# A gated cross-attention block on one core: values laid out by token in device memory, scores laid out by head and query

## The reference

```python
def attention(hidden_q, hidden_kv, mask, bias, Wq, Wk, Wv, Wo):   # 32 heads of 128
    q, k, v = (hidden_q @ Wq, hidden_kv @ Wk, hidden_kv @ Wv)     # reshaped to b, 64, 32, 128
    score = einsum('bqhd,bkhd->bhqk', q, k) / sqrt(128) + bias
    probs = softmax(where(mask, score, -inf));  probs = where(mask, probs, 0)
    return einsum('bhqk,bkhd->bqhd', probs, v).reshape(b, 64, 4096) @ Wo

x = x + tanh(g_xattn) * attention(layernorm(x), ctx, ...)
x = x + tanh(g_ffn) * ffn(layernorm(x), ...)   # ffn: low-rank scores choose one of each 32
                                               # hidden units (1792 in all), relu, product with w2t
```

## Time and profile before

| | |
|---|---|
| median of 3 runs | 1898.65 us (1897.91 to 1899.12) |
| the profiled execution | 1899.45 us, span 1897.7 us |
| mean granted clock of TensorE | 0.992 of full |
| busy: PE, PEld, DVE, ACT, POOL | 98%, 84%, 58%, 37%, 50% |
| bytes moved by DMA | 329.88 MB in 185,597 packets |
| loads of kt, qt (2048 KB each), 16 of each | 8.9 us and 13.8 us from issue to landing |
| loads of v (512 KB each), 64 | 11.2 us from issue to landing |

### The profile page before, as it was taken

How to read it: one execution, slowest core, us unless ns; L and a number is a source line. 1 busy time by engine, 2 the same in 40 slices (tenths; PEclk the granted TensorE clock), 3 DMA queues, 4 the chain that set the end, 5 groups by cost and what they waited for, 6 DMA issues and landing times. The chain is left out here.

```text
span 1897.7 us, 37889 instructions
## 1 busy us (share of the span) xinstructions
PE 1853.6 (98%) x15304; PEld 1594.9 (84%) x15304; DVE 1095.4 (58%) x1748; ACT 698.7 (37%) x1773; POOL 958.0 (50%) x762
## 2 busy tenths in 40 slices
PE   8999999999999999999989999999999889999999
PEld 7899988799998888888868888888888668888887
DVE  5333466333355455334357777877777877777673
ACT  4233333322233333333345555555555432222221
POOL 5666688766668788778723232323323432111110
PEclk9999999999999999999999999999999999999999
DMA  5555665644455554467679998799985430000000
GB/s 178 168 179 170 194 207 187 200 161 152 144 184 188 189 189 166 166 225 244 200 232 319 294 254 249 221 319 307 253 263 144 131 122 23 23 23 27 25 17 17
DMA packets 185597, 329.88 MB, mean 174 GB/s; under 512 B 11856, under 2 KB 118480, under 8 KB 176464
## 3 DMA queue, kind: packets, MB, share of 16 engines
q1 hardware_dynamic: 185424, 327.47, 54.9%
HBM read 214.17 MB, written 113.25 MB: 173 GB/s over the span
## 5 line engine op out<-in xcount | busy, mean ns | idle before, releaser
L1409 PE MATMUL bank<-tokens_hi,wkq_hi 128*128 128x512 f32 x888 | 347.1, 391 | 4.9 <-DVE tokens_lo L1014 3.3
L1410 PE MATMUL bank<-tokens_lo,wkq_hi 128*128 128x512 f32 x888 | 345.8, 389 | 0.0
L1411 PE MATMUL bank<-tokens_hi,wkq_lo 128*128 128x512 f32 x888 | 345.8, 389 | 0.0
L685 POOL TENSOR_TENSOR wkq_lo<-raw_wkq,wkq_hi 128x768 fp32r<-128x768 f32 x126 | 284.1, 2274 | 122.0 <-ACT wkq_hi L791 121.7
L1409 PE MATMUL bank<-wv_s_hi,tokens_hi 128*128 128x256 f32 x896 | 255.6, 285 | 4.1 <-POOL wv_s_lo L685 4.1
L1410 PE MATMUL bank<-wv_s_lo,tokens_hi 128*128 128x256 f32 x896 | 254.8, 284 | 0.0
L1411 PE MATMUL bank<-wv_s_hi,tokens_lo 128*128 128x256 f32 x896 | 254.7, 284 | 0.0
L1409 PE MATMUL bank<-wo_hi,attn_t_hi 128*128 128x512 f32 x512 | 207.6, 405 | 12.3 <-DVE attn_sum L1208 7.2
L1411 PE MATMUL bank<-wo_hi,attn_t_lo 128*128 128x512 f32 x512 | 201.4, 393 | 0.0
L1409 PEld LDWEIGHTS bank<-tokens_hi,wkq_hi 128*128 128x128 f32 x888 | 166.7, 188 | 40.7 <-issue 4.7
L1410 PE MATMUL bank<-wo_lo,attn_t_hi 128*128 128x512 f32 x512 | 200.9, 392 | 0.0
(11 more groups left out here) (145 smaller groups left out, 3729.1 us busy)
## 6 DMA issues: line engine op xcount, KB each, us to landing
k_t<-c SPq DMA_DIRECT2D x128, 256.0 KB, 2.4
v_by_head<-c SPq DMA_DIRECT2D x128, 256.0 KB, 2.2
q_t<-c SPq DMA_DIRECT2D x128, 256.0 KB, 2.4
kt<-k_t SPq DMA_DIRECT2D x16, 2048.0 KB, 8.9
qt<-q_t SPq DMA_DIRECT2D x16, 2048.0 KB, 13.8
v<-v_by_head SPq DMA_DIRECT2D x64, 512.0 KB, 11.2
raw_wkq<-in_wk SPq DMA_DIRECT2D x32, 512.0 KB, 4.0
raw_wv<-in_wv SPq DMA_DIRECT2D x16, 1024.0 KB, 5.6
```

The costliest lines, as they stand in the source:

```text
L685: pool.tensor_tensor(lo, job_raw(r)[:, a:b, :], hi.bitcast(F32), ALU.subtract)\
L1409: pe.matmul(o, a[0], b[0], start=first_mm, stop=False, skip_group_check=not grouped)
L1410: pe.matmul(o, a[0], b[1], start=False, stop=False, skip_group_check=not grouped)
L1411: return pe.matmul(o, a[1], b[0], start=False, stop=last_mm, skip_group_check=not grouped)
```

## The change

The values lie in device memory by token (`v_by_token`): for each iteration 128 rows (token of a pair) of 8 pairs x 4 heads x 128 float32, 16 KB in a row. One DMA loads an iteration. For that, the score tile is laid out anew: its partitions are (one of two heads, query of a batch), and its columns (couple of heads, batch of the pair, key). The transposes then give partitions (batch, key), which is a token. The bias is laid out accordingly on input. The mask now depends on the column and, for both heads, the query; it comes as three inputs: by row (for the row factor) and by query for each half. Since the two heads of a partition share a query but the two batches do not, the row factor no longer fits the partition: it is multiplied into the gate of the final sum instead (`gate_valid`). The order of score and value matmuls follows the layout; their number and sizes are the same. In SP's order the mask loads come behind a wait for the stores of the normalised tokens, in whose buffer's place the new mask tiles lie; `mask_add[1]` takes the place of `mask_rows` and of its own input `mask_in[1]`.

```diff
-    v_d = nc.dram_tensor("v_by_head", [ITERS, PPH, P, 2, 2, DH], F32, kind="Internal").ap()
+    v_d = nc.dram_tensor("v_by_token", [ITERS, P, PPH, 2, 2 * DH], F32, kind="Internal").ap()
...
-        mask_add = at("mask_add", [P, PAIRS, S], BF16, 0.5)
+        mask_add = [at(f"mask_add{i}", [P, PPH, 2, S], BF16, (204, 0.5)[i]) for i in range(HALVES)]
-        mask_in = at("mask_in", [P, PAIRS, S], U8, 206)
+        mask_in = [at(f"mask_in{i}", [P, PPH, 2, S], U8, (206, 205)[i]) for i in range(HALVES)]
+        mask_rows = at("mask_by_row", [P, PAIRS, S], U8, 204)
...
@@ store @@
-                    dst = v_d[half * G + u // 2, t:t + 2, :, i].rearrange("t q h d -> q t (h d)")
+                    dst = v_d[half * G + u // 2, :, t:t + 2, i, :]
@@ load_v @@
-                for h in range(2):
-                    for i in range(2):
-                        sp.dma_start(v[it % 2][h * S:(h + 1) * S, :, :, i, :].rearrange("k p b d -> k (p b) d"),
-                                     v_d[it][:, :, i, h, :].rearrange("p (b k) d -> k (p b) d", b=2))\
-                            .then_inc(v_in[it % 2], 16)
+                sp.dma_start(v[it % 2][:, :, :, :], v_d[it].rearrange("q t i e -> q t (i e)"))\
+                    .then_inc(v_in[it % 2], 16)
@@ SP, n == 83 @@
-                    sp.dma_start(mask_in[:, :, :], mask).then_inc(mask_sem, 16)
+                    sp.wait_ge(xn_out, 16 * PAIRS)
+                    sp.dma_start(mask_rows[:, :, :], mask[:, 0:PAIRS * S].rearrange("p (t k) -> p t k", k=S))\
+                        .then_inc(mask_sem, 16)
+                    for i in range(HALVES):
+                        ...
@@ ACT @@
-                hi = cxo[d % 2][0][:, :, :, :].rearrange("p a (r h) t -> p h a r t", h=2)[:, h]
+                hi = cxo[d % 2][0][:, :, :, h * S:(h + 1) * S]
...
-                if n == 90:
+                if n == 86:
                     act.wait_ge(gate_sem, 16)
                     act.activation(gate[:, :], gate_in[:, :], ACT.Tanh).then_inc(act_gate, 1)
@@ masks @@
-                dve.wait_ge(mask_sem, 16)
-                dve.tensor_scalar(mask_add[:, :, :], mask_in[:, :, :], -MASKED, MASKED, ALU.mult, ALU.add)\
-                    .then_inc(dve_mask, 1)
-                dve.tensor_reduce(valid[:, :], mask_in[:, :, :], AX.X, ALU.max).then_inc(dve_mask, 1)
+                dve.wait_ge(mask_sem, 48)
+                dve.tensor_reduce(valid[:, :], mask_rows[:, :, :], AX.X, ALU.max).then_inc(dve_mask, 1)
+                dve.tensor_scalar(mask_add[1][:, :, :, :], mask_in[1][:, :, :, :], -MASKED, MASKED,
+                                  ALU.mult, ALU.add).then_inc(dve_mask, 1)
+                dve.wait_ge(dve_mask, 2)
+                dve.tensor_scalar(mask_add[0][:, :, :, :], mask_in[0][:, :, :, :], -MASKED, MASKED,
+                                  ALU.mult, ALU.add).then_inc(dve_mask, 1)
+                dve.wait_ge(act_gate, 1)
+                dve.tensor_scalar(gate_valid[:, :], valid[:, :], gate[:, 0:1], None, ALU.mult).then_inc(dve_mask, 1)
@@ probs, DVE @@
-                dve.scalar_tensor_tensor(
-                    out=sc[s % 2][:, :, :], in0=sc[s % 2][:, :, :], scalar=valid[:, tile:tile + 1],
-                    in1=rinv[s % 2][:, :].unsqueeze(2).broadcast_to([P, HG, S]),
-                    op0=ALU.mult, op1=ALU.mult).then_inc(dve_p, 1)
+                dve.tensor_tensor(sc[s % 2][:, :, :], sc[s % 2][:, :, :],
+                                  rinv[s % 2][:, :].unsqueeze(2).broadcast_to([P, HG, S]), ALU.mult)\
+                    .then_inc(dve_p, 1)
@@ scores, PE @@
-                    for h in range(HG):
-                        o = (s % 2 * HG + h) * S
-                        for q in range(2):
-                            cols = slice(p * P + q * S, p * P + (q + 1) * S)
-                            mm = pe.matmul(bank[SCORE_BANK[r % 2]][q * S:(q + 1) * S, o:o + S],
-                                           qt[it % 2][:, h, cols], kt[it % 2][:, h, cols], start=True, stop=True)
+                    for r_ in range(2):
+                        for b in range(2):
+                            cols = slice(p * P + b * S, p * P + (b + 1) * S)
+                            o = (s % 2 * HG + 2 * r_ + b) * S
+                            for h in range(2):
+                                mm = pe.matmul(bank[SCORE_BANK[r % 2]][h * S:(h + 1) * S, o:o + S],
+                                               qt[it % 2][:, 2 * r_ + h, cols], kt[it % 2][:, 2 * r_ + h, cols],
+                                               start=True, stop=True)
@@ attend, PE @@
-                for b in range(2):
-                    for r in range(2):
-                        o = (s % 2 * 4 + 2 * r + b) * S
-                        for i in range(4):
-                            a, h = divmod(i, 2)
-                            keys = slice(h * S, (h + 1) * S)
...
+                for h in range(HG):
+                    o = (s % 2 * HG + h) * S
+                    for i in range(4):
+                        a, b = divmod(i, 2)
+                        keys = slice(b * S, (b + 1) * S)
...
```

More of the change, by code:

```diff
@@ L173, in build @@
         valid = tiny("row_has_key", [P, PAIRS], F32, 64)
+        gate_valid = tiny("gate_if_key", [P, PAIRS], F32, 64)
         m1 = tiny("block_max", [P, NBLK], F32, 224)
@@ L203, in build @@
         qt = [at(f"qt{i}", [P, HG, 2 * TB], F32, (20, 76)[i]) for i in range(2)]
-        v = [at(f"v{i}", [P, PPH, 2, 2, DH], F32, (36, 92)[i]) for i in range(2)]
+        v = [at(f"v{i}", [P, PPH, HG, DH], F32, (36, 92)[i]) for i in range(2)]
         bias_in = [at(f"bias_in{i}", [P, PPH, HG * S], F32, (52, 108)[i]) for i in range(2)]
@@ L593, in _ @@
                     sp.dma_start(gate_in[:, :], gates).then_inc(gate_sem, 16)
-                    sp.dma_start(mask_in[:, :, :], mask).then_inc(mask_sem, 16)
+                    sp.wait_ge(xn_out, 16 * PAIRS)
+                    sp.dma_start(mask_rows[:, :, :], mask[:, 0:PAIRS * S].rearrange("p (t k) -> p t k", k=S))\
+                        .then_inc(mask_sem, 16)
+                    for i in range(HALVES):
+                        o = (i + 1) * PAIRS * S
+                        sp.dma_start(mask_in[i][:, :, :, :],
+                                     mask[:, o:o + PAIRS * S].rearrange("p (t b k) -> p t b k", b=2, k=S))\
+                            .then_inc(mask_sem, 16)
                 if n == 86:
@@ L701, in do_bm @@
                 if s == 0:
-                    pool.wait_ge(dve_mask, 2)
+                    pool.wait_ge(dve_mask, 4)
                 if p == 0:
                     pool.wait_ge(*loaded(bias_sem, it))
[L705 to L708, removed]
+                b = bias_in[it % 2][:, p, :].rearrange("p (r k) -> p r k", r=2)
+                m = mask_add[it // G][:, p, :, :].rearrange("p b k -> p (b k)")
+                pool.tensor_tensor(b, b, m.unsqueeze(1).broadcast_to([P, 2, 2 * S]), ALU.add).then_inc(pool_bm, 1)
             def do_lo(n):
@@ L1106, in probs @@
             def probs(s):
-                it, p = divmod(s, PPH)
-                tile = PPH * (it // G) + p
                 dve.wait_ge(act_exp, s + 1)
@@ L1189, in clo @@
                 dve.wait_ge(act_chi, 2 * d + h + 1)
-                hi, lo = (t[:, :, :, :].rearrange("p a (r h) t -> p h a r t", h=2)[:, h] for t in cxo[d % 2])
-                dve.tensor_tensor(lo, bank[PV_BANK[h]][:, :].rearrange("p (a r t) -> p a r t", a=2, r=2),
+                hi, lo = (t[:, :, :, h * S:(h + 1) * S] for t in cxo[d % 2])
+                dve.tensor_tensor(lo, bank[PV_BANK[h]][:, :].rearrange("p (a h q) -> p a h q", a=2, q=S),
                                   hi.bitcast(F32), ALU.subtract).then_inc(dve_clo, 1)
@@ L1211, in add_wo @@
                     dve.wait_ge(dve_wo, s + 1)
-                    dve.scalar_tensor_tensor(out=acc[:, p, :], in0=acc[:, p, :], scalar=gate[:, 0:1],
+                    dve.scalar_tensor_tensor(out=acc[:, p, :], in0=acc[:, p, :], scalar=gate_valid[:, tile:tile + 1],
                                              in1=xres[tile % 2][:, :], op0=ALU.mult, op1=ALU.add)\
@@ L1301, in finish @@
                     .then_inc(dve_o, 1)
-            dve.wait_ge(act_gate, 1)
+            dve.wait_ge(dve_mask, 4)
             for d in range(DUOS + 3):
@@ L1503, in attend @@
                     pe.wait_ge(dve_clo, s)
-                for b in range(2):
-                    for r in range(2):
-                        o = (s % 2 * 4 + 2 * r + b) * S
-                        for i in range(4):
-                            a, h = divmod(i, 2)
-                            keys = slice(h * S, (h + 1) * S)
-                            dims = slice(a * S, (a + 1) * S)
-                            mm = pe.matmul(bank[PV_BANK[h]][dims, o:o + S], v[it % 2][keys, p, b, r, dims],
-                                           pt[keys, s % 2, r, b, :], start=True, stop=True)
+                for h in range(HG):
[3 more added lines that the diff above has]
```

(13 more changed lines are left out.)

8 lines of the change are left out of this document (4 added, 4 removed).

## The result

After: 1901.26 us median of 21 runs (1898.02 to 1904.16); before, beside them on the same chip: 1898.65 (1895.66 to 1900.42). The ratio is 1.0017 [1.0011, 1.0023]: the change costs 2.6 us, where the forecast was a gain of 2.0. The profiled execution took 1901.21.

A forecast was written before the change was run, and what follows sets the result against it. TensorE, busy 98% of the span, was taken as the bound, so only less matmul work or shorter seams pay. -1.97 - 0.15 + 0.1 = -2.0 us from the 1898.65 median gave 1896.6, called "same"; stated range 1891.5 to 1902.

The forecast's parts named there:

- Masks at unit 88: VectorE's added mask work ahead of u2 and u3, about +0.9 us there, stalls TensorE 0 to 0.3: +0.1 taken.
- The slack of 0.9: At unit 88, u3 could end about 0.9 us later before TensorE's matmuls would have to wait.
- +0.6 for writing in place: At unit 88, 0.6 us more if the mask product writing over its own input's place ran at half speed.
- Holes, -1.97: Two gaps in the value matmuls near 1290, read as late instructions during DMA backlog, would go: -1.97 us.
- Rival A: The gaps in the value matmuls near 1290 stay: 1898.6 us; chance 0.21.
- C: Late instructions become more frequent in the value matmuls while v flows in 16 KB packets: about 1912 us; chance 0.11.
- D: The new order of score matmuls does not overlap in pairs, +74 us: about 1970; chance 0.03.
- Row factor, -0.15: Probabilities product (L1112) without its per-partition factor: 0.06 us less each, -0.15 for TensorE at the seams.
- B: The last seam, after 1500, shortens too, with less wait for the attention sum: about 1892 us; chance 0.18.
- The middle one: Seam at 1250 to 1300: VectorE's x-tile wait stays, as v is not ahead of it in SP's queue: 0.
- Stores, score and value matmuls, 0: Stores of v land well before their buffer is reused; score and value matmuls keep number and alternation: 0 each.
- slower: The outcome of a measurably slower kernel: chance 0.16, made of C, D and 0.02.

The follow-up runs named there:

- masks apart: Kernel after with the mask work behind u3, second product and gate_valid in unit 89: 1898.01 us against 1899.02 before, ratio 0.9994.
- reduction first: Kernel before with only the reduction put ahead of its one mask product: a single run of 1900.29 us.
- GpSimd in pieces: Kernel after with GpSimd's subtractions in units 86 to 92 cut into pieces of 128x256: 1898.8 us, ratio 1.0 to before.

## Why the prediction was wrong

**Failed: "Masks at unit 88", +0.1 forecast, +4.87 measured.** I priced the second product at the 0.69 of the first, and the 128x16 one with its wait at 0.2: a block of 2.19 + 0.9 = 3.1. It is 6.25. The slack of 0.9 that I had worked out was right: 6.25 - 2.19 = 4.06 later, less 0.9, is 3.2, and TensorE's next matmul came 3.16 late; the second expense, 1.7 at the lower clock behind the idle, I hadn't thought of. What was missing is that the one row I took the price from the earlier trace rows was a lucky one, placed between two operations of GpSimd, and that the change moves the products off that place by putting the reduction ahead of them. I never read GpSimd's rows there, and bounded the term only by a +0.6 for writing in place, which neither product does. The Trainium skill (SBUF — State Buffer, SBUF: two separate sides, and Who interferes with whom) has the rule: VectorE and GpSimd share a port pair, held for a whole instruction; a tensor_scalar in a two-port mode and a GpSimd operation block each other fully, a tensor_reduce and ScalarE are outside it. The traces agree as far as they show it: products that end half a microsecond behind GpSimd's operations, reductions of 1.22 in every kernel, 1.05 on ScalarE. The mode that a product runs in stands in no row.

**Holes, -1.97: right in kind, smaller as a rule.** Transposes of the kernel after, where two duos had taken 18.41 us:

```profile
1291.49 0.66 PE L1499 MATMUL bank<-ident,scores 128*128 128x128 f32 x4
...
1299.71 0.66 PE L1499 MATMUL bank<-ident,scores 128*128 128x128 f32 x4
```

8.22. None of the eight profiled executions with v in 16 KB runs has a hole there, while the four with loads by head had 2.2, 0.7, 0.4 and 0. The execution I read had the most; their mean, 0.8, is my estimate of what the change takes away. The one with 512 B runs by token (share 0.76) had none either. That the backlog of DMA makes them remains a reading: the kernel with 256 B runs had the highest share and none. Rival A is out as to the holes, C because no new ones came, and D because the duos are 8.22 apart.

**Row factor, -0.15: right in the size of the operation, too small to see in the time.** The group of VectorE in the kernel after, answering to the earlier trace rows:

```profile
L1120 DVE TENSOR_TENSOR scores<-scores,rowinv 128x256 f32<-128x256 f32 x128 | 59.2, 462 | 4.4
```

0.058 off each, 0.06 forecast; the waits for it went from 2.3 to 2.2, and to 3.1 with the factor put back.

**Seams.** The last one kept its 7.2, so B is out. The first, which the sum left out, came 0.7 shorter. Its longest duo is 4.2 to 4.3 above the 8.22 in the five executions whose stage begins at 967.1 or later, and 4.8 where one can be read that begins earlier; the kernel before with more masks is among the five, so it isn't the layout, and a late start seems to win some of its delay back there. The middle one, forecast unchanged, came 1.0 shorter too, and the wait of 0.9 that was to stay is gone: the x tile was waited for 3.12 instead of 3.57, as VectorE's row shows. Over the kernels with the x tiles where they were, its long duo is 0.4 to 2.7 above the rest, shortest in the two executions of the kernel after (0.7, 0.4). Some of unit 88's delay may be given back there too: it is 4.9 long, and taking it away brought 3.6 to 4.4 (each kernel against the one before beside it: 1.0 and 1.8 below, 2.6 above). But the kernel before with more masks has the same delay and a long duo of 1.8, and the one with 512 B runs 1.2, so the delay alone doesn't do it. Why this seam is shorter stays open.

```profile
1252.85 0.75 DVE L1219 SCALAR_TENSOR_TENSOR attn_sum<-attn_sum,gate_if_key,x_tile 128x512 f32<-128x512 f32 x1 [3.12 <-DMA x_tile<-in_x]
```

**Stores, score and value matmuls, 0: right** (2.3 us to landing; duos of 8.22). **Chances**: the time lay inside the range by luck, in a part that was put there for C and for the last seam, neither of which came; "slower" had 0.16, all of it on C and mishaps, none on VectorE, the only engine with work added ahead of a wait. With the block at 6.25 the sum is -0.8 - 0.15 + 4.87 = +3.9, and with the seams as they came, -0.7 and -1.0, +2.2, against +2.6 measured.

## What to carry to other kernels

Before a VectorE operation is priced from one row, look at what GpSimd runs at that moment, and where the new copy will fall: the same product cost 0.69 between two GpSimd operations and 2.77 behind one. Place such work behind the operation that TensorE waits for, or on ScalarE, or cut GpSimd's operations: each of the three took the loss back (3.6, 3.8 to 4.4, and 2.8 us). A load that halves its DMA time is worth nothing where no matmul waits for it (share 0.89 to 0.68 over the stage, some 0.8 us).

## What the runs showed of the hardware

- A 128x1024 uint8 to bf16 product on VectorE: 0.69 us between two operations of GpSimd; 0.97 to 2.77 when it came during a GpSimd subtraction of 0.75 to 2.83 us. It ended 0.54 to 0.56 us behind the GpSimd operation that it met, in each of seven meetings in four kernels (the kernel after, masks apart, reduction first, GpSimd in pieces). A 128x16 product took 0.69 to 0.71 in each kernel and ended 0.02 to 0.04 behind an operation of GpSimd where that was looked up. GpSimd loses as well: its two subtractions took 4.63 with the meetings, 4.20 without.
- TensorE's 3.0 us of idle at unit 88 cost another 1.7 at the lower clock level.
- Loads of v flowing alone: 431 GB/s in 16 KB runs over 128 partitions (991 to 996, kernel after), 278 in 512 B runs over 128, 204 and 169 in 512 and 256 B runs over 64. The Trainium skill (SBUF — State Buffer, Door 1: The DMA port swizzle) says that partitions 0 to 63 reach only half of the ports and gives 196 GB/s measured for them. The 199 of the earlier trace rows agrees; that the ports are what set it here no run separates.
